# Cross attention on one NeuronCore: the probabilities' transposition moved from TensorE to VectorE and a DRAM buffer

## The reference

```python
q = norm((ln(x) @ Wq).reshape(b, 32, 16, 128))
k = norm((ctx @ Wk).reshape(b, 257, G, 128))
v = (ctx @ Wv).reshape(b, 257, G, 128)
p = softmax(q @ k.T / sqrt(128), axis=-1)
out = (p @ v).reshape(b, 32, 2048) @ Wo
x = x + out
```

## Time and profile before

| | |
|---|---|
| median of three runs | 3686.31 us (3679.96 to 3687.12) |
| the profiled execution | 3681.27 us |
| its span | 3679.5 us, 75523 instructions |
| busy TensorE, matmuls | 3373.0 us (92%) |
| busy TensorE, weight loads | 2261.3 us (61%), beside the matmuls |
| busy VectorE | 2266.2 us (62%) |
| busy ScalarE | 1870.3 us (51%) |
| busy GpSimd | 77.7 us (2%) |
| mean granted clock of TensorE | 0.971 |
| DMA | queue q1 12.5% of 16 engines' span; HBM 40 GB/s |

### The profile page before, as it was taken

The page is one execution under the profiler, slowest core; times in us unless marked ns, Lnnn a source line. Parts: engine busy times, 40 slices in busy tenths (PEclk is TensorE's granted clock), DMA queues, the critical chain, the costliest instruction groups (busy, mean ns, idle before and its releaser), DMA issues. The chain is left out here.

```text
span 3679.5 us, 75523 instructions
## 1 busy us (share of the span) xinstructions
PE 3373.0 (92%) x25760; PEld 2261.3 (61%) x25760; DVE 2266.2 (62%) x5629; ACT 1870.3 (51%) x5129; POOL 77.7 (2%) x132
## 2 busy tenths in 40 slices
PE   7999999999998989978886899999999999987799
PEld 4666666666662335556674567667667676665555
DVE  4555555555552227668886677777777777767732
ACT  5656556566544653345563554554554555534421
POOL 0000000000000000000000000000000000000000
PEclk9999999999998999999998999999999999998899
DMA  4111111111112020000002111111111111101000
GB/s 137 52 43 51 43 43 51 43 52 50 45 36 75 1 97 34 11 3 6 6 4 87 39 41 44 36 44 44 36 46 44 36 44 43 38 30 49 1 9 14
DMA packets 117807, 147.98 MB, mean 40 GB/s; under 512 B 11968, under 2 KB 95552, under 8 KB 116032
## 3 DMA queue, kind: packets, MB, share of 16 engines
q1 hardware_dynamic: 117696, 146.54, 12.5%
HBM read 138.91 MB, written 7.60 MB: 40 GB/s over the span
## 5 line engine op out<-in xcount | busy, mean ns | idle before, releaser
L436 PE MATMUL x_Kb<-x_cT,x_wk 128*128 128x257 f32 x3072 | 766.8, 384 | 15.7 <-ACT x_sq L698 8.5
L436 PEld LDWEIGHTS x_Kb<-x_cT,x_wk 128*128 128x128 f32 x3072 | 554.5, 191 | 172.7 <-issue 83.7
L473 PE MATMUL x_PC<-x_pT,x_cn 128*128 128x512 f32 x1024 | 475.1, 607 | 4.1 <-DVE x_oT L1012 0.8
L718 ACT ACTIVATE x_pr<-x_pr,x_ntop 128x257 f32<-128x257 f32 x512 | 261.1, 510 | 298.3 <-DVE x_ntop L968 157.6
L698 ACT ACTIVATE x_sq<-x_Kb 128x257 f32<-128x257 f32 x512 | 195.3, 382 | 311.3 <-DVE x_kT L951 305.7
L473 PEld LDWEIGHTS x_PC<-x_pT,x_cn 128*128 128x128 f32 x1024 | 185.0, 191 | 244.0 <-issue 242.0
L951 DVE TENSOR_SCALAR x_kT<-x_Kb,x_vecs 128x257 f32<-128x257 f32 x512 | 245.7, 483 | 75.2 <-PE x_Kb L436 68.8
L455 PE MATMUL x_Sb<-x_kT,x_qT 128*32 128x257 f32 (+1 forms) x4096 | 275.7, 383 | 4.9 <-DVE x_pr L971 3.3
L724 ACT ACTIVATE x_pr<-x_pr,x_rps 128x257 f32<-128x257 f32 x512 | 240.3, 499 | 41.1 <-DVE x_rps L981 40.8
L988 DVE COPY x_pT<-x_PTb 128x512 f32<-128x512 f32 x256 | 176.8, 691 | 119.4 <-PE x_PTb L465 117.4
L1002 DVE SCALAR_TENSOR_TENSOR x_pcT<-x_last,x_cT,x_PC 128x512 f32<-128x512 f32 x256 | 190.3, 745 | 85.4 <-PE x_PC L473 81.2
(11 more groups left out here) (313 smaller groups left out, 5966.1 us busy)
## 6 DMA issues: line engine op xcount, KB each, us to landing
x_cT<-in_ctxT SPq DMA_DIRECT2D x128, 257.0 KB, 2.8
x_cn<-in_ctx SPq DMA_DIRECT2D x128, 256.0 KB, 3.0
x_last<-x_last_row SPq DMA_DIRECT2D x128, 256.0 KB, 3.8
e_w<-in_e_w SPq DMA_DIRECT2D x3, 1152.0 KB, 7.8
c_staged_heads<-in_c_wqk SPq DMA_DIRECT2D x2, 1536.0 KB, 9.7
x_wq<-in_x_wq SPq DMA_DIRECT2D x1, 2048.0 KB, 8.1
x_wo<-in_x_wo SPq DMA_DIRECT2D x1, 2048.0 KB, 13.3
x_last_row<-x_last_rows SPq DMA_DIRECT2D x128, 2.0 KB
```

The costliest lines, as they stand in the source:

```text
L436: m = pe.matmul(Kb[j % 2][:, 0:SE], wk[:, c, g * HD:(g + 1) * HD], cT[:, b, c, :], start=c == 0, stop=c == HC - 1)
L473: m = pe.matmul(PC[h][:, :], cn[:, b, c, h * P:(h + 1) * P], pT[:, c, :], start=c == 0, stop=c == KC - 1)
L718: act.activation(pr[:, v, :], pr[:, v, :], ACT.Exp, bias=ntop[:, u:u + 1], scale=1.0 if L1 else -1.0, accum_out=ps[:, u:u + 1]).then_inc(e ...
```

## The change

The probabilities are no longer turned by TensorE. VectorE turns each unit in blocks of 32x32, `turned[:, :, v*32:(v+1)*32]` from `pr[:, v, 0:256]`: two units ahead of the scaling of scores 2 of their own slot, the other two a slot later, where the first copy of `pT` stood. A block transposition leaves the four blocks of a unit on their own 32 partitions, so what must still be moved is moved across partitions: SyncE stores the four bands of 32 partitions into the DRAM buffer `probs_row` (four stores of 32x8x128) and fetches `pT` from it in one piece. The columns of `pT` then stand by key head first, which makes the operands of `project_values` and of `project_value_pair` runs of 128 and changes the layout of the last row. The bank `PTb` goes. The context rows `cn` have two buffers in place of four, with a load and a semaphore of their own (`load_context_rows`), and TensorE waits for both before the weighing. The diff, cut to what the steps need:

```diff
@@ -132,6 +132,7 @@
         last_row = nc.dram_tensor(n + "last_row", [2, UNITS * P], F32, kind="Internal").ap()
+        probs_row = nc.dram_tensor(n + "probs_row", [KC * 4, S, 4, UNITS * S], F32, kind="Internal").ap()
         if L1:
@@ -170,7 +171,7 @@
         qT = sb("qT", [P, BT, NH, S])
-        cn = sb("cn", [P, BT, KC, H])
+        cn = sb("cn", [P, 2, KC, H])
         cT = sb("cT", [P, BT, HC, SE])
@@ -181,6 +182,7 @@
         rps = sb("rps", [P, BT * UNITS])
+        turned = sb("turned", [P, KC * 4, UNITS * S])
         pT = sb("pT", [P, KC, UNITS * P])
@@ -200,7 +202,6 @@
         Sb = [bank("Sb0"), bank("Sb1")]
-        PTb = bank("PTb")
         PC = [bank("PC0"), bank("PC1")]
@@ -341,16 +344,33 @@
                              ).then_inc(ctx_in[b].sem, 16)
-                sp.dma_start(cn[:, b, :, :], d["ctx"][i * BT + b][0:LAST, :].rearrange("(c p) n -> p c n", p=P)
-                             ).then_inc(ctx_in[b].sem, 16)
+
+            def load_context_rows(i, b, wait=True):
+
+                if wait:
+                    sp.wait_ge(pc_done.sem, pc_done.after(i, HC * (b - 1)))
+                sp.dma_start(cn[:, b % 2, :, :], d["ctx"][i * BT + b][0:LAST, :].rearrange("(c p) n -> p c n", p=P)
+                             ).then_inc(cn_in[b % 2].sem, 16)
+
+            def store_probs(i, b):
+
+                sp.wait_ge(pt_turned.sem, pt_turned.now(i, 2 * (b + 1)))
+                for a in range(4):
+                    sp.dma_start(probs_row[:, :, a, :].rearrange("m k n -> k m n"), turned[S * a:S * (a + 1), :, :]
+                                 ).then_inc(pt_stored.sem, 16)
+
+            def fetch_probs(i, b):
+
+                sp.wait_ge(pt_stored.sem, pt_stored.now(i, b + 1))
+                sp.dma_start(pT[:].rearrange("p c (a n) -> p c a n", a=4),
+                             probs_row.rearrange("(c j) k a n -> (j k) c a n", c=KC)).then_inc(pt_moved.sem, 16)
 
...
                 sp.wait_ge(last_turned.sem, last_turned.now(i, b + 1))
-                sp.dma_start(last_row[b % 2].rearrange("(v a q) -> a v q", v=UNITS, a=4),
-                             last_rows[S - 1:P:S, :].rearrange("a (v q) -> a v q", v=UNITS)
+                sp.dma_start(last_row[b % 2].rearrange("(a n) -> a n", a=4), last_rows[S - 1:P:S, :]
                              ).then_inc(last_sent.sem, 16)
@@ -367,7 +387,11 @@
                         load_out_weights(1)
+                    store_probs(i, b)
                     send_last(i, b, nxt)
+                    fetch_probs(i, b)
+                    if (b + 1 < BT or nxt) and not (first and b == 0):
+                        load_context_rows(i + (b + 1) // BT, (b + 1) % BT)
                     if b == 0 and not first:
@@ -456,21 +483,15 @@
 
-            def transpose_probs(t, b, p):
-                pe.wait_ge(pn_done.sem, pn_done.now(t, UNITS * b + 2 * p + 2))
-                pe.wait_ge(pt_copied.sem, pt_copied.after(t, 2 * b + p))
-                for v in range(2):
-                    for c in range(KC):
-                        at = v * KC + c
-                        m = pe.transpose(PTb[:, at * P:(at + 1) * P], pr[:, 2 * p + v, c * P:(c + 1) * P], ident[:])
-                m.then_inc(pt_done.sem, 1)
-
             def weigh_context(t, b):
-                pe.wait_ge(pt_copied.sem, pt_copied.now(t, 2 * (b + 1)))
+                pe.wait_ge(pt_moved.sem, pt_moved.now(t, b + 1))
+                pe.sem_inc(gate, 1)
+                pe.wait_ge(cn_in[b % 2].sem, cn_in[b % 2].now(t, b // 2 + 1))
+                pe.sem_inc(gate, 1)
                 pe.wait_ge(pc_copied.sem, pc_copied.after(t, HC * b))
...
                     for c in range(KC):
-                        m = pe.matmul(PC[h][:, :], cn[:, b, c, h * P:(h + 1) * P], pT[:, c, :],
+                        m = pe.matmul(PC[h][:, :], cn[:, b % 2, c, h * P:(h + 1) * P], pT[:, c, :],
                                       start=c == 0, stop=c == KC - 1)
@@ -478,20 +499,19 @@
                     for c in range(HC):
-                        w = pcT[:, c, 0, :].rearrange("p (j a q) -> p a j q", j=J, a=4)[:, g]
-                        m = pe.matmul(PC[0][:, g * P:(g + 1) * P].rearrange("p (j q) -> p j q", j=J),
-                                      wv[:, c, g * HD:(g + 1) * HD], w, start=c == 0, stop=c == HC - 1)
+                        m = pe.matmul(PC[0][:, g * P:(g + 1) * P], wv[:, c, g * HD:(g + 1) * HD],
+                                      pcT[:, c, 0, g * P:(g + 1) * P], start=c == 0, stop=c == HC - 1)
                 m.then_inc(v_done.sem, 1)
...
                 for z in range(NG):
-                    wide = PC[z][:, :].rearrange("p (b a j q) -> p a b j q", b=2, a=4, j=J)
+                    wide = PC[z][:, :].rearrange("p (b a n) -> p a b n", b=2, a=4)
                     for a in range(4):
...
                         for c in range(HC):
-                            w = pcT[:, c, :, z * J * P:(z + 1) * J * P].rearrange("p b (j a q) -> p a b j q", j=J, a=4)
-                            m = pe.matmul(wide[:, a], wv[:, c, g * HD:(g + 1) * HD], w[:, a],
+                            w = pcT[:, c, :, a * P + z * J * S:a * P + (z + 1) * J * S]
+                            m = pe.matmul(wide[:, a], wv[:, c, g * HD:(g + 1) * HD], w,
                                           start=c == 0, stop=c == HC - 1)
@@ -575,9 +595,6 @@
                         project_key(i, s, g)
-                    if g in (LEAD, LEAD + 2):
-                        for t, b in back(i, s, 1, cur, prev):
-                            transpose_probs(t, b, g // 2)
                     if g == 1 and s == 0 and nxt:
@@ -955,7 +972,7 @@
                 dve.wait_ge(k_rs.sem, k_rs.now(t, b * NG + y + 1))
-                dve.wait_ge(pt_done.sem, pt_done.after(t, 2 * (b - 1) + v // 2 + 1))
+                dve.wait_ge(pt_turned.sem, pt_turned.after(t, 2 * (b - 1) + v // 2 + 1))
                 if v == 0:
@@ -980,13 +997,16 @@
 
-            def copy_probs(t, b, p):
-                dve.wait_ge(pt_done.sem, pt_done.now(t, 2 * b + p + 1))
+            def turn_probs(t, b, p):
+
+                dve.wait_ge(pn_done.sem, pn_done.now(t, UNITS * b + 2 * p + 2))
                 if p == 0:
+                    dve.wait_ge(pt_moved.sem, pt_moved.after(t, b))
+                else:
                     dve.wait_ge(pc_done.sem, pc_done.after(t, HC * b))
-                    dve.wait_ge(pc_copied.sem, pc_copied.after(t, HC * b))
-                dve.tensor_copy(pT[:, :, 2 * p * P:2 * (p + 1) * P].rearrange("k c (v r) -> k v c r", v=2),
-                                PTb[:, :].rearrange("k (v c r) -> k v c r", v=2, c=KC)).then_inc(pt_copied.sem, 1)
+                for v in (2 * p, 2 * p + 1):
+                    w = dve.transpose(turned[:, :, v * S:(v + 1) * S], pr[:, v, 0:LAST])
+                w.then_inc(pt_turned.sem, 1)
 
@@ -1090,11 +1110,10 @@
                         copy_key(i, s, g)
-                    if g in (LEAD, LEAD + 2):
+                    if g == LEAD:
                         for t, b in back(i, s, 1, cur, prev):
-                            copy_probs(t, b, g // 2)
-                            if g == LEAD:
-                                turn_last(t, b)
+                            turn_probs(t, b, 1)
+                            turn_last(t, b)
                     if g == 0 and s == 0 and nxt:
@@ -1155,6 +1174,7 @@
                 if cur:
+                    turn_probs(i, s, 0)
                     shift_scores(i, s, 2)
```

More of the change, by code:

```diff
@@ L221, in cross_attention @@
         gate = ctx.semaphore(n + "gate")
-        ctx_in = [sig(f"context_loaded{b}", 1, 16 * 2) for b in range(BT)]
+        ctx_in = [sig(f"context_columns_loaded{b}", 1, 16) for b in range(BT)]
+        cn_in = [sig(f"context_rows_loaded{j}", 2, 16) for j in range(2)]
         ln_sum = sig("ln_stats", 1)
@@ L253, in cross_attention @@
         pn_done = sig("probs_normed", BT * UNITS)
-        pt_done = sig("probs_transposed", BT * 2)
-        pt_copied = sig("pT_copied", BT * 2)
+        pt_turned = sig("probs_turned_in_blocks", BT * 2)
+        pt_stored = sig("probs_stored", BT, 16 * 4)
+        pt_moved = sig("probs_moved", BT, 16)
         last_turned = sig("last_probs_turned", BT)
@@ L321, in _ @@
                          ).then_inc(key_weights, 16)
-            for s in ctx_in:
+            for s in ctx_in + cn_in + [pt_stored, pt_moved]:
                 s.prime(sp)
@@ L377, in _ @@
             load_context(0, 0)
+            load_context_rows(0, 0, False)
             if not L1:
@@ L386, in _ @@
                 load_context(0, b)
+                if b == 1:
+                    load_context_rows(0, 1, False)
             tile(0, True, True)
@@ L397, in _ @@
         def _(pe):
-            for s in (xt_done, q_done, qt_done, k_done, ss_done, s_done, pt_done, pc_done, v_done, y_done):
+            for s in (xt_done, q_done, qt_done, k_done, ss_done, s_done, pc_done, v_done, y_done):
                 s.prime(pe)
@@ L842, in _ @@
```

(2 more changed lines are left out.)

## The result

| | before | changed |
|---|---|---|
| median | 3683.14 us (4 runs) | 3741.97 us (4 runs, 3738.21 to 3747.40) |
| ratio | | 1.0162, 95% interval 1.0141 to 1.0183 |
| span of the profiled execution | 3679.5 us | 3738.2 us |

What follows compares the result with a forecast made beforehand. TensorE was taken to set the pace. Layer 0's slots 1 to 3 -31, its slot 0 +13, layer 1 -3, drains +9 and semaphores +4 summed to -8 us: 3673 profiled, 3678 us as median, range 3635 to 3730.

Steps and rivals of the forecast that it cites:

- The turning of units 0 and 1 costs nothing: Layer 1: it lies in VectorE's wait for the key scales, 10.7 us a tile; without that cover, 45 us.
- -3 us: Layer 1: key 4 starts 0.07 us earlier in 48 slots; the rest of TensorE's freed time becomes waiting.
- 0.9 us more: Layer 0, slot 0: TensorE waits for the next tile's tokens, delayed by VectorE's turnings; 15 x 0.9 = +13 us.
- The wait for the tokens: Layer 0, slot 0: TensorE waits 2 us or more for the normalised tokens, where it idled 0.56 us.
- Freed time, 0.43 us a group: TensorE: each of 256 groups of transpositions occupies 0.43 us, so at most 110 us leave it.
- The key ring in layer 0: Slots 1 to 3: two PSUM banks make keys wait for ScalarE's squares, leaving 0.65 us a slot, -31 us.
- The extra waits and increments: TensorE ahead of each weighing: two waits and two increments more, 0.03 us each time, +4 us, bounds 0 to 13.
- The way through DRAM: SyncE's stores and fetch after the turning take 7.2 us, hidden in the loop by 8.0 us in the shortest slot.
- The drains, +9 us: End of each layer: nothing covers the way through DRAM, +3.8 us in layer 0 and +5.6 in layer 1.
- the trip decides: Rival, chance 0.19: a longer DRAM way delays layer 0's slot 3 weighing; 3710 us at 10 us, 3828 at 12.
- VectorE decides: Rival, chance 0.18: transpositions cost 0.44 us apart instead of 0.35, or their strided output more; 3694 us and more.
- TensorE's time comes back in full: Rival: key rings have slack and tokens come in time; 3585 us, half of it 3635; full or half 0.17.

Runs made afterwards that it cites:

- the changed kernel shifted: The changed kernel with 70 tiny writes of VectorE ahead of layer 1's loop; 3705.14 us, ratio 1.0063.
- the kernel before shifted: The kernel before with 60 tiny writes of VectorE ahead of layer 1's loop; 3712.42 us, ratio 1.0080.
- With the wait cut to 1.2 us: The changed kernel with the next tokens normalised ahead of the turning of units 2 and 3 in layer 0; 3719.00 us, ratio 1.0099.
- the run with all cures: The changed kernel with tokens first, one turning a pair, third key bank, context rows loaded with the columns; 3616.84 us, ratio 0.9815.
- With one wait ahead of the weighing: The changed kernel with the context rows loaded with the columns, as before, without the two increments; 3735.09 us, ratio 1.0148.
- the run that has neither side effect: The changed kernel with tokens first in layer 0 and one turning instruction a pair, still two key banks; 3679.47 us, ratio 0.9991.
- the third bank: The changed kernel with a third PSUM bank for the keys, in place of the turned probabilities' bank; 3693.79 us, ratio 1.0032.
- the same order of the tokens on both sides: The kernel before with tokens normalised ahead of the first copy of the probabilities in layer 0; 3666.44 us, ratio 0.9959.

## Why the prediction was wrong

**What failed first: a cost that the sum did not have.** "The turning of units 0 and 1 costs nothing" and "-3 us" for layer 1 took the instructions as the only cost. They lengthen VectorE's code: 57 more instructions ahead of its loop of layer 1, and 8 more in it, put the loop where its code no longer stays loaded. That is 37 us by one run (the changed kernel shifted) and 30 by the other (the kernel before shifted). The second has the loop at its old length, so the place is enough; what the 8 do is not shown. Without the loading my term nearly holds: the tile of layer 1 was to be within 0.3 of 79.4, and it is 79.00 to 79.04, some 5 us less in the layer where I had 3.

**What failed second: "0.9 us more" in slot 0 of layer 0, +13 us.** The wait for the tokens was forecast well, 2 us or more, and 2.22 came. In the tiles in which the clock held, slot 0 takes 18.0 us, which is 1.05 more than 16.95: the step was right. But I priced an idle TensorE at its idle time, and in 8 tiles out of 12 the clock went to its 1.2 GHz level behind the wait and cost 1.65 us more, 8 x 1.65 = 13 us in this execution. With the wait cut to 1.2 us the clock held in every tile.

**The other terms.** From 3678 to 3742 us are 64. The loading has 37 of them, the clock 13, slots 1 to 3 of layer 0 some 12 (the ring and the extra waits below), and slot 0 without the clock, the drains and layer 1 together some 2. The tile of layer 0 was to be 1 us shorter; with the clock held it is 67.0 us against 66.95 before.
- Freed time, 0.43 us a group: right where it can be read alone, by the 0.89 and 0.85 us a slot of the run with all cures. The busy time of 154.2 us and the 127.8 of the weight loads would both have been too much.
- The key ring in layer 0, 0.65 us a slot, -31 us: half came. Slots 1 to 3 lost 0.17, 0.37 and 0.48 us, 1.02 a tile in place of 1.95. With one wait ahead of the weighing they lost 0.56, 0.52 and 0.54: so 0.6 a tile was the waits', and the ring took 0.1 more of a slot than I had it take.
- The extra waits and increments, 0.03 us each, +4: too small, and outside my bounds of 0 and 13 by a little. They cost 0.2 to 0.4 us ahead of three weighings in four of layer 0, 0.15 ahead of one in four of layer 1, 14 us together.
- The way through DRAM, 7.2 us against a slack of 8.0: it is 7.5 to 7.8, and 0.56 us remain. Hidden, as forecast; doubling the stores showed where it ends.
- The drains, +9 us: the last intervals of weighings grew from 8.66 to 13.90 and from 6.87 to 13.13 us, +5.2 and +6.3.

The rival "the trip decides" is refuted by its own mark: the waits for pT stand in the drains, and in the loop there is one of 0.9 us. So is "VectorE decides": the turnings take 420 ns, and the tile of layer 1 is shorter once the code stays loaded. The advice of the Trainium skill that I weighed beside that rival (VectorE: DVE Perf Modes, Rules for kernel authors), TensorE for full transpositions, came out right in sign for this pair of kernels, but not by the length of the turnings; with the third bank and the other cures the sign is the other one. "TensorE's time comes back in full" did not come true in any run: with the ring opened and every cure the kernel is at 3616.8 us against the 3585 of that rival, and 15 us of its gain are the tokens'. That is half of the 101 us. My sum of 3678 us agrees with the run that has neither side effect (3679.5) by luck, with errors that cancel: the key ring and the waits too hopeful, and some 11 to 15 us from the earlier tokens that the sum did not hold.

## What to carry to other kernels

Before an instruction is added to a long loop, look at the engine's count of instructions in that loop and at the packets of the code queues: a loop whose code just fits can tip over through some 60 instructions ahead of it, and then every turn pays at its top. Idle time of TensorE can cost more than its length: read the granted clock behind the longest wait. When an engine is relieved, open the ring that it waits on in the same change; here the bank that the removed step set free was worth 48 to 52 us, and the removal without it nothing (a loss of 13 us with the same order of the tokens on both sides).

## What the runs showed of the hardware

- **Code loading.** In the loops that load, the page's queue q14 moves 8 KB packets, five in each turn, and VectorE stops for 2.2 to 2.6 us at the top, in 12 turns of each of the seven kernels that load (2.25 to 2.4 in the changed one). Of the five one begins 1.0 us behind the branch and one at the end of the stop, 3.4 us behind it; by the order of the trace the other three begin near instructions 59, 176 and 307 of the 332, 117 and 131 apart. So I estimate some 128 instructions for one packet. The Trainium skill (Advanced Engine Details and Errata, ISA Cache) has 32 KB in two lines of 16 KB, 256 instructions each. By that page's line I estimate 128 instructions in 8 KB, and the distances of the loads agree. The size would fit: a loop that lies in four blocks of 8 KB and reaches for a fifth finds none left. The lines don't: here the packets are 8 KB. That four blocks fit is argued from these counts, not shown.
- **Two loops of nearly one length.** A loop of 324 instructions ran without loading and, 60 instructions further on, with it; one of 332 loaded, and 70 instructions further on did not. The free places, 1879 and 2006, are 127 apart, which fits blocks of 128 but doesn't prove them.
- **The clock.** At the 1.2 GHz level a key record follows its predecessor after 0.43 us instead of 0.22. A wait of 2.2 us in layer 0 was followed by it 8 times of 12 (10 of 12 in the shifted kernel), one of 2.6 to 2.8 us in layer 1 3 times of 12, and one of 2.5 us in the shifted kernel before once in 12. What decides between them is open.
- **Waits on TensorE.** One further wait and two increments ahead of a weighing cost together 0.15 to 0.4 us where they showed at all (slots 0 to 2 of layer 0, slot 3 of layer 1), with nothing shown that ended the idle time.
